# Operands of VectorE's long comparisons and products moved to PSUM, and a vector added by TensorE, in a four-layer graph network

## The chip, the cores and the metric

The kernel runs on one core of one Trainium2 chip. A core has five engines with their own instruction queues: TensorE (PE in the profile; PEld is its weight load), VectorE (DVE), ScalarE (ACT), GpSimd (POOL) and SyncE (SP). SBUF is the working memory of 128 partitions, PSUM the memory of eight banks that TensorE writes and that VectorE and ScalarE can read and write. The metric is the device time of one execution in microseconds (us); lower is better.

## The reference

Four layers of a graph network over 6250 nodes with 128 features and 100,000 edges. Edges are sorted by destination, and both ends and the relation of an edge are data of the run. Each layer takes `h = relu(layernorm(x))` and adds its result to `x`:

```python
# L0: weighted sum of the sources' rows
x = x + (1 + eps) * h + segment_sum(h[src] * edge_weight[:, None], dst)
# L1: three rounds of a gated graph convolution
h1 = relu(h @ W_node + b_node); w = (z * edge_attr).sum(1)
for i in range(3):
    agg = segment_sum(w[:, None] * (h1 @ conv[i])[src], dst)
    h1 = gru_cell(agg, h1, ...)
x = x + h1
# L2: a weight matrix per relation (16), scaled by one attention value per relation
alphas = sigmoid(relu(erps @ attn_w1 + attn_b1) @ attn_w2 + attn_b2)
vrps = zeros.at[dst].add(alphas[rels] * (h @ w_rel)[rels, src])
x = x + relu(vrps.at[dst].add((h @ update)[dst]))
# L3: mean over the edges by source (the same edges, grouped by their other end)
x = x + (h + segment_sum(h[dst], src) / max(deg, 1)) @ W.T + b
```

## The kernel before

The edges lie in 782 tiles of 128 edges (784 with padding, `ET`), the nodes in 49 blocks of 128 (`BLK`). An aggregation is a *pass*: for each tile GpSimd issues one indirect DMA that fetches the 128 source rows into one of 64 ring slots of `G` (`gather`, L709). VectorE builds a 128 x 128 selection matrix `M` from the tile's destinations (`build`, L1260 and L1262), TensorE multiplies `M` with the rows (`mm`, L813), and VectorE adds the product to the accumulator's block (`one_round`, L1282). A tile that touches two blocks takes two steps, so a pass has 832 steps in 26 rounds of 32 (`NRD`, `RD`). Every 64th tile is not gathered by GpSimd: SP fetches its 128 rows one by one (L576), so GpSimd issues 770 gathers in a pass and 780 in the last. There are six passes, one after the other: L0, three of L1 (called passes 1, 2 and 3 here), L2 and L3. Between them lie dense stages (layer norm, gates), which need the whole of a pass and give the rows that the next one gathers.

GpSimd, at every fourth tile `t`, waits until the rows of tile `t + 3 - 32` have landed (SP counts the landings, L587) and until TensorE has done step `t - 12` of the pass, which frees the ring slot (`gather_pass`). TensorE, in its queue's order, waits for SP's count, for `M` and for a free PSUM bank (banks 0 to 3).

The passes of L1 and L2 carry extra work for later layers, put between the steps by hand (`extra(r, u)`, `u` the step in its round):

- Pass 1, `place`, 98 blocks of 8 tiles, one every 8 steps. VectorE compares the chunk numbers of an iota (`srow`) with the edges' (`hs_t`) into one-hots of 128 x 392 (`one_hots`, L1429, at `u % 8 == 0`). TensorE multiplies them with a triangle to rank each edge among its like (`place`, at `u % 8 == 3`, PSUM bank 4 or 5). At `u % 8 == 6` VectorE adds the tiles' first numbers `Qb` (L1446), multiplies by the one-hots (L1448), and reduces (L1449). ScalarE's queue loads `Qb` for block `j` with one DMA that repeats a row of 392 numbers over 128 partitions (L1883), issued when VectorE has released the buffer of block `j - 2`.
- Passes 2 and 3, `places`: for every 4 tiles four comparisons of `irow`, an iota, with the numbers `hi_f` and `lo_f`, 128 x 256 each (L1457); seven times, `chunk_places` compares and multiplies in pieces of 128 x 400 (L1470, L1472).
- L2, `attention`: for 16 tiles at a time, the relations are compared with `srow[:, 0:16]` (L1602), multiplied by `alpha` (L1603) and reduced (L1604).

Of the kernel before, what the change touches and what calls it, by code (L numbers as in the profile page):

```python
# [5 lines left out]
ALU = mybir.AluOpType  # L6
# [7 lines left out]
P = 128  # L14
# [7 lines left out]
BLK = -(-N // P)  # L22
PAD_NODE = BLK * P - 1
R, B = 16, 8
# [18 lines left out]
RD = 32  # L43
NRD = S // RD
# [25 lines left out]
PB = 8  # L70
# [19 lines left out]
PASS_PLACE = PASS_L1  # L90
PASS_ORDER = {PASS_L1 + 1: (0, 4), PASS_L1 + 2: (4, NB)}
SORT_AT = 1
PLACE_AT = 1
KEY3_AT, LIST3_AT, LAST_AHEAD = 8, 14, 22
XT, XC = 3 * GN, 4
LN0, N0, G0, G1, G2, N2, N3 = range(7)
# [14 lines left out]
def gnn_kernel(nc, a, out):  # L111
# [4 lines left out]
    with ExitStack() as ctx:  # L116
        def sb(name, shape, dt=F32):
            return ctx.enter_context(nc.sbuf_tensor(name, shape, dt))
# [16 lines left out]
        ps = ctx.enter_context(nc.psum_tensor("ps", [P, 8, BANK], F32))  # L135
# [3 lines left out]
        irow = sb("irow", [P, P])  # L139
        srow = sb("srow", [P, SW])  # L140
# [175 lines left out]
        rows3 = sorting[0:T3_TB, 4 * QA * R:4 * QA * R + T3_NB * P].rearrange("p (b c) -> p b c", b=T3_NB)  # L316
        ix3_i = gate[:, 0:T3].bitcast(I32)
        adiag = sb("adiag", [R, R])
        alpha = sb("alpha", [P, R])
        note = sb("note", [P, 16])  # L320


# [13 lines left out]
        s_tr = sem("s_tr")  # L336
# [468 lines left out]
        def _(pe):  # L805
# [6 lines left out]
            def mm(dst, lhsT, rhs, start=True, stop=True):  # L812
                return nc.tensor.matmul(dst, lhsT, rhs, start=start, stop=stop, skip_group_check=True)  # L813
# [137 lines left out]
            def place(r, u):  # L951

                v = u // PB
                j = (r - PLACE_AT) * (RD // PB) + v
                if u % PB == 3 and not (isinstance(j, int) and j >= PLACES):
                    pe.wait_ge(s_oh, j + 1)
                    mm(ps[:, 4 + v % 2, 0:PB * BLK], before_b[:], oh[:, v % 2, :]).then_inc(s_rk, 1)

            def order(i, rr, u):

# [93 lines left out]
                last = mm(ps[0:R, 5, 0:D], erT[0:w, c, :], aw1[0:w, c, :], start=c == 0, stop=c == 2)  # L1054
            last.then_inc(s_tr, 1)
            unit()
            mm(ps[:, 4, 64:64 + R], ones[0:R, :], adiag[:]).then_inc(s_tr, 1)
            gather_pass(PASS_L2, 0, KEY3_AT, W1)
            staircase(2, 6, T3_TB, T3_NB, S3)
            unit()  # L1060
# [44 lines left out]
        def _(dve):  # L1105
# [160 lines left out]
            def lead_in(k, of, weight):  # L1266
                for s in range(LEAD):
                    build(k, s, s, of, weight)
# [109 lines left out]
            def lanes(t, n, m):  # L1378
                return t.rearrange("s (b c) -> s b c", c=1).broadcast_to((n, t.shape[1], m))
# [44 lines left out]

            def one_hots(j, v):
                hs = hs_t[:, bass.ds(j * PB, PB)].rearrange("p (k c) -> p k c", c=1).broadcast_to((P, PB, BLK))
                of = srow[:, 0:BLK].rearrange("p (k c) -> p k c", k=1).broadcast_to((P, PB, BLK))
                to = oh[:, v % 2, :].rearrange("p (k c) -> p k c", k=PB)
                V.tensor_tensor(to, of, hs, ALU.is_equal).then_inc(s_oh, 1)  # L1429

            def place(r, u):
                i = r - PLACE_AT
                v = u // PB
                j = i * (RD // PB) + v
                if u == 0:
                    link.turn(i, 8)
                if isinstance(j, int) and j >= PLACES:
                    return
                if u % PB == 0:
                    one_hots(j, v)  # L1440
                if u % PB == 6:
                    half = v % 2
                    at = pq[:, half, :]
                    dve.wait_ge(s_rk, j + 1)
                    dve.wait_ge(s_qld[half], 16 * (i * (RD // PB // 2) + v // 2 + 1))
                    V.tensor_tensor(at, ps[:, 4 + half, 0:PB * BLK], Qb[:, half, :], ALU.add).then_inc(s_pl, 1)  # L1446
                    dve.wait_ge(s_pl, j + 1)
                    link(V.tensor_tensor(at, at, oh[:, half, :], ALU.mult))  # L1448
                    link(V.tensor_reduce(pos_f[:], at.rearrange("p (k c) -> p k c", k=PB), AX.X, ALU.add))  # L1449
                    V.tensor_copy(pos[:, bass.ds(j * PB, PB)], pos_f[:]).then_inc(s_pos, 1)  # L1450

            def places(j, q):

                row = irow[:].rearrange("p (k c) -> p k c", k=1).broadcast_to((P, 2, P))
                for t, to, done in ((hi_f, hi_m, s_hi), (lo_f, lo_m, s_lo)):
                    for k in range(0, B4, 2):
                        ins = V.tensor_tensor(to[:, q, k:k + 2], row, lanes(t[:, bass.ds(j * B4 + k, 2)], P, P),  # L1457
                                              ALU.is_equal)
                    ins.then_inc(done, 1)
# [28 lines left out]
            for l in range(LAYERS):  # L1488
                k = PASS_L1 + l
                if k == PASS_L1 + 1:  # L1490
                    link(V.tensor_single_scalar(lo_i, pos[:], P - 1, ALU.bitwise_and))
                    V.tensor_copy(lo_f, lo_i)
                    link(V.tensor_single_scalar(pos[:], pos[:], 7, ALU.logical_shift_right))
                if k in PASS_ORDER:
                    link(V.tensor_copy(hi_f, pos[:]))
                    j = PASS_ORDER[k][0] * (TB // B4)
                lead_in(k, rel, w_l)
                if k in PASS_ORDER:
                    if j:
# [6 lines left out]
                if k == PASS_PLACE:  # L1506
                    gather_pass(k, 0, PLACE_AT, *args)
                    gather_pass(k, PLACE_AT, NRD, *args, place)
                    link.part(NRD - 1 - PLACE_AT, 8, 4)
                else:  # L1510
                    def order_and_relation(r, u, k=k):
                        order(PASS_ORDER[k][0] // 2 + r // HALF, r % HALF, u, PASS_ORDER[k][1] * (TB // B4))
                        if k == PASS_L1 + 2:
                            relation(r, u)
                            if r == FEED and u == 0:

                                link(V.tensor_copy(src_f, ix_src[:, 0:ET]))
                                link(V.scalar_tensor_tensor(ix_t, src_f, float(R), rl[:], ALU.mult, ALU.add))
                                signal(s_ix)

                    for r in range(NRD):
                        one_round(k, r, RD if r < NRD - 1 else RD - LEAD, *args, order_and_relation)
                    link.leave(1, link.k)
# [66 lines left out]
            dve.wait_ge(s_att, 2)  # L1590
            ready(V.tensor_scalar(adiag[:], ident[0:R, 0:R], alog[:, 1:2], None, ALU.mult))
            unit_done()
            link(V.tensor_copy(alpha[:], ps[:, 4, 64:64 + R]))
            link.leave(1, link.k)

            def attention(q, to):

                at = bass.ds(q * QA, QA)

                def over(t):  # L1600
                    return t.rearrange("p (s r) -> p s r", s=1).broadcast_to((P, QA, R))
                link(V.tensor_tensor(by_rel[:, to], lanes(rl[:, at], P, R), over(srow[:, 0:R]), ALU.is_equal))  # L1602
                link(V.tensor_tensor(by_rel[:, to], by_rel[:, to], over(alpha[:]), ALU.mult))  # L1603
                V.tensor_reduce(a_l[:, at], by_rel[:, to], AX.X, ALU.add).then_inc(s_aw, 1)  # L1604

            def attention_ahead(r0):
# [114 lines left out]
        def _(act):  # L1721
# [150 lines left out]
            for l in range(LAYERS):  # L1872
                ph = G0 + l
                if PASS_L1 + l == PASS_PLACE:

                    act.wait_ge(s_qrdy, 1)
                    act.dma_start(q_flat.rearrange("(b p h) -> p b h", p=TB, h=BLK), Q).then_inc(s_qst, 16)
                    act.wait_ge(s_qst, 16)
                    q_of = q_flat.rearrange("(j c) -> j c", c=PB * BLK)
                    for j in range(PLACES):  # L1880
                        if j >= 2:
                            act.wait_ge(s_pl, j - 1)
                        act.dma_start(Qb[:, j % 2, :], q_of[j:j + 1, :].broadcast_to((P, PB * BLK))) \  # L1883
                            .then_inc(s_qld[j % 2], 16)
                        if (j - 6) % 7 == 0 and 0 <= (j - 6) // 7 < NG:
                            hn_out(0, (j - 6) // 7)
                elif PASS_L1 + l == PASS_L1 + 1:
                    act.wait_ge(s_hs[1], two_stores(1, G0))
                    def every_eighth(j):
                        if j % 8 == 4 and j >= 12 and (j - 12) // 8 < NG:  # L1890
                            hn_out(1, (j - 12) // 8)

                    for v in range(*PASS_ORDER[PASS_L1 + l]):
                        order(v // 2, v % 2, every_eighth)
                elif PASS_L1 + l == PASS_L1 + 2:
                    act.wait_ge(s_hs[1], two_stores(1, G1))
                    done = []

                    def some(j):
                        n = j - PASS_ORDER[PASS_L1 + 2][0] * (TB // B4) - 12  # L1900
                        if n >= 0 and n % 8 == 0 and n // 8 < NG:
                            hn_out(2, n // 8)
                            done.append(n // 8)
                    for v in range(*PASS_ORDER[PASS_L1 + l]):
                        order(v // 2, v % 2, some)
                    for i in range(len(done), NG):
                        hn_out(2, i)
                    act.wait_ge(s_hnd, 16 * NG * LAYERS)
# [97 lines left out]
```

## Time and profile before

| | |
|---|---|
| three timed runs, us | 6528.85, 6530.85, 6519.95; median 6528.85 |
| profiled execution, first to last instruction (span) | 6527.6 us |
| GpSimd busy | 4763.4 us, 73% of the span |
| VectorE busy | 3826.2 us, 59% |
| TensorE busy | 3347.2 us, 51% |
| mean granted TensorE clock | 0.598 of full speed |

Of the profiled execution the page gives the span alone; no other time of it is listed. The busy time of an engine holds no waits, and issue of DMAs by SP and ScalarE is not counted as busy. "issue" in the chain of waits is time in which an engine waited for nothing that the profile shows.

### The profile page before, as it was taken

The page shows a single profiled execution, that of the slowest core. Times are in us where ns is not written, and L with a number is a line of the kernel's source. Part 1 is how long each engine was busy: PE and PEld are TensorE (multiplying, and loading weights), DVE is VectorE, ACT ScalarE, POOL GpSimd, SP SyncE. Part 2 cuts the span into 40 slices and gives each one's busy share as a digit, 9 for nine tenths or more (in the row PEclk, how much of TensorE's full clock was granted, in tenths as well). Part 3 has the DMA queues.
Part 4 walks back from the last instruction along what each step waited for, and adds up shares of the span by engine and source line. Part 5 has one row for each costly group of instructions (what it writes and reads, how often), then busy time and mean ns, then how long its engine had stood idle before and what let it go on. Part 6 is the DMA issues. An engine that isn't in the chain of part 4 may idle for free.

```text
span 6527.6 us, 107309 instructions
## 1 busy us (share of the span) xinstructions
PE 3347.2 (51%) x13560; PEld 2696.1 (41%) x13560; DVE 3826.2 (59%) x13371; ACT 878.1 (13%) x2206; POOL 4763.4 (73%) x5006
## 2 busy tenths in 40 slices
PE   3444445444446555555755554595454444444444
PEld 3333334333334445554454543443343333333334
DVE  6767676666666656666666664454454444444445
ACT  1000001000002111111311110143333333000000
POOL 6777776777774677777777777675777776777775
PEclk6555556555556766667767675696555555555556
DMA  5434432333332222222222222253222222222222
GB/s 141 110 107 111 111 108 78 79 78 78 81 78 76 55 57 58 57 57 58 67 57 58 57 57 59 79 222 123 54 54 53 54 54 55 54 54 55 54 55 59
DMA packets 287231, 491.20 MB, mean 75 GB/s; under 512 B 100950, under 2 KB 183899, under 8 KB 280268
## 3 DMA queue, kind: packets, MB, share of 16 engines
q0 software_dynamic: 156176, 306.05, 19.2%
q1 hardware_dynamic: 89707, 94.69, 4.4%
q10 hardware_dynamic: 40656, 83.51, 4.2%
q14 instruction: 535, 4.37, 0.2%
q8 instruction: 157, 2.57, 0.2%
HBM read 398.97 MB, written 86.91 MB: 74 GB/s over the span
## 4 chain that ended last, share of the span: by engine, by line
POOL 41%; issue 20%; DMA 13%; SPq 11%; PE 10%; DVE 3%; ACT 1%; DVEq 1%; POOLq 0%; ACTq 0%
POOL G L709 40%; DMA G<-h_rows,ix_src 10%; PE ps L813 10%; SPq L576 8%; SPq L568 3%; DMA G<-h_rows 1%; DMA G<-t_rows,pos 1%; DMA t_rows<-G 0%; DVEq L1271 0%; PE ps L875 0%; DVE HNA L1282 0%; ACT gate L1920 0%; SPq L587 0%; DVE bst L1199 0%; ACT gate L1828 0%
## 5 line engine op out<-in xcount | busy, mean ns | idle before, releaser
L709 POOL DMA_INDIRECT G<-h_rows,ix_src x3860 | 3699.8, 958 | 1284.2 <-issue 1044.2
L813 PE MATMUL ps<-G,M 128*128 x10000 | 2558.9, 421 | 3014.0 <-SPq L587 2140.6
L813 PEld LDWEIGHTS ps<-G,M 128*128 128x128 f32 x10000 | 2171.0, 310 | 3402.6 <-issue 3397.3
L1282 DVE TENSOR_TENSOR HNA<-HNA,ps 128x128 f32 (+1 forms) x3328 | 959.0, 288 | 1349.1 <-PE ps L813 1313.8
L1262 DVE TENSOR_SCALAR M<-irow,rel,w_l 128x128 f32<-128x128 f32 x3328 | 1207.9, 365 | 184.0 <-issue 177.5
L709 POOL DMA_INDIRECT G<-t_rows,pos x770 | 739.6, 961 | 260.7 <-issue 227.3
L1282 DVE TENSOR_TENSOR HTA<-HTA,ps 128x129 f32 x840 | 243.5, 290 | 518.2 <-PE ps L813 509.5
L1865 ACT ACTIVATE sorting<-sorting,pk 128x128 f32<-128x128 f32 x784 | 250.4, 390 | 1433.2 <-DVE sorting L1457 1432.4
L813 PE MATMUL ps<-sorting 128*128 128x128 f32 x1568 | 438.2, 376 | 2.0 <-issue 1.3
L1960 ACT ACTIVATE G<-G,pk 128x128 f32<-128x128 f32 x782 | 311.9, 402 | 676.6 <-DMA G<-t_rows,pos 676.1
L1282 DVE TENSOR_TENSOR X<-X,ps 128x128 f32 x832 | 239.3, 288 | 232.4 <-PE ps L813 222.5
L813 PEld LDWEIGHTS ps<-sorting 128*128 128x128 f32 x1568 | 369.6, 290 | 3.3 <-issue 3.2
L1260 DVE TENSOR_SCALAR M<-irow,rel 128x128 f32<-128x128 f32 x832 | 259.9, 317 | 49.5 <-issue 48.9
L1260 DVE TENSOR_SCALAR M<-irow,hs_t 128x128 f32<-128x128 f32 x840 | 256.7, 306 | 52.5 <-issue 51.8
L734 POOL DMA_INDIRECT by_src<-chunks,cix x224 | 226.4, 1011 | 74.1 <-issue 68.2
L813 PE MATMUL ps<-big,HTA 128*128 128x512 f32 x392 | 190.9, 618 | 10.0 <-DVE G L1561 10.0
L1852 ACT COPY HG<-ps 128x512 f32<-128x512 f32 (+1 forms) x39 | 21.5, 551 | 1047.1 <-DVE sorting L1446 883.5
L1753 ACT ACTIVATE HG<-X,nbias,rstd 128x128 f32<-128x128 f32 x74 | 30.6, 486 | 967.7 <-POOL nbias L727 967.7
L1824 ACT COPY gate<-ps 128x512 f32<-128x512 f32 (+1 forms) x26 | 14.5, 558 | 1008.4 <-PE ps L875 1008.4
L1457 DVE TENSOR_TENSOR sorting<-irow,hs_t 128x256 f32<-128x256 f32 x392 | 148.5, 420 | 0.0
L1457 DVE TENSOR_TENSOR sorting<-irow,gate 128x256 f32<-128x256 f32 x392 | 148.3, 420 | 0.2
L1561 DVE COPY G<-ps 128x512 f32<-128x512 f32 x98 | 67.8, 692 | 124.1 <-PE ps L813 95.2
(271 smaller groups left out, 2200.2 us busy)
## 6 DMA issues: line engine op xcount, KB each, us to landing
G<-h_rows SPq DMA_DIRECT2D x7680, 0.5 KB
G<-h_rows,ix_src POOLq DMA_INDIRECT x3860
t_rows<-G SPq DMA_DIRECT2D x49, 1024.0 KB, 4.1
HTA<-in_edge_attr_n ACTq DMA_DIRECT2D x50, 500.0 KB
HTA<-in_edge_attr ACTq DMA_DIRECT2D x50, 500.0 KB
G<-t_rows SPq DMA_DIRECT2D x1536, 0.5 KB
sorting<-q_flat ACTq DMA_DIRECT2D x98, 196.0 KB
G<-t_rows,pos POOLq DMA_INDIRECT x770
```

Source lines behind the costliest of these rows:

```text
L568: _, row = nc.values_load_multi_w_load_instructions(listed[32 * j:32 * j + 1, bass.ds(c * P + q * ROWS_A_QUAD, RD)], engines=[mybir.Engine ...
L576: sp.dma_start(G[e:e + 1, BY_ROW + j % 2, 0:D], table[bass.ds(row[e % RD], 1), :]) \
L709: return nc.gpsimd.indirect_dma_start(to, None, table, bass.IndirectOffsetOnAxis(ap=ix, axis=0))
L734: nc.gpsimd.indirect_dma_start(by_src, bass.IndirectOffsetOnAxis(ap=cix[:, c:c + 1], axis=0), chunks[:, v, k * CH:(k + 1) * CH], None).the ...
L813: return nc.tensor.matmul(dst, lhsT, rhs, start=start, stop=stop, skip_group_check=True)
L1260: ins = V.tensor_scalar(M[:, slot, :], irow[:], at, None, ALU.is_equal)
L1262: ins = V.tensor_scalar(M[:, slot, :], irow[:], at, weight[:, bass.ds(s, 1)], ALU.is_equal, ALU.mult)
L1282: V.tensor_tensor(to, to, ps[:, u % SLOTS, 0:n], ALU.add).then_inc(s_add, 1)
L1457: ins = V.tensor_tensor(to[:, q, k:k + 2], row, lanes(t[:, bass.ds(j * B4 + k, 2)], P, P), ALU.is_equal)
L1561: V.tensor_copy(t_buf[t % 2][:, c * BANK:(c + 1) * BANK], ps[:, 6, :]).then_inc(s_te[1], 1)
L1865: ins = A.mul(to, to, pk[:, bass.ds(j * B4 + k, 1)])
L1960: A.mul(G[:, slot, 0:D], G[:, slot, 0:D], a_l[:, bass.ds(turn * RING + u, 1)]) \
```

## The change

Constants that VectorE compared with or multiplied by from SBUF are copied to PSUM once before the pass, and the long operations read them there. In `place` the addition of `Qb` by VectorE goes: TensorE adds it with a second matrix product, of a row of ones with the one row of 392 numbers, into the same PSUM bank; the product with the one-hots then reads PSUM. `Qb` is loaded into one partition. The wait for its landing moves from VectorE to TensorE, and the signal that releases its buffer now comes with the product.

```diff
+L2_IOTA, L2_ALPHA = 448, 480
-        alpha = sb("alpha", [P, R])
@@ TensorE, place
                     pe.wait_ge(s_oh, j + 1)
-                    mm(ps[:, 4 + v % 2, 0:PB * BLK], before_b[:], oh[:, v % 2, :]).then_inc(s_rk, 1)
+                    pe.wait_ge(s_qld[v % 2], 16 * ((r - PLACE_AT) * (RD // PB // 2) + v // 2 + 1))
+                    mm(ps[:, 4 + v % 2, 0:PB * BLK], before_b[:], oh[:, v % 2, :], stop=False)
+                    mm(ps[:, 4 + v % 2, 0:PB * BLK], ones[0:1, :], Qb[0:1, v % 2, :], start=False).then_inc(s_rk, 1)
@@ TensorE, before L2's pass
-            mm(ps[:, 4, 64:64 + R], ones[0:R, :], adiag[:]).then_inc(s_tr, 1)
+            mm(ps[:, 7, L2_ALPHA:L2_ALPHA + R], ones[0:R, :], adiag[:]).then_inc(s_tr, 1)
@@ VectorE, one_hots
-                of = srow[:, 0:BLK].rearrange("p (k c) -> p k c", k=1).broadcast_to((P, PB, BLK))
+                of = ps[:, 7, 0:BLK].rearrange("p (k c) -> p k c", k=1).broadcast_to((P, PB, BLK))
@@ VectorE, place
-                    dve.wait_ge(s_qld[half], 16 * (i * (RD // PB // 2) + v // 2 + 1))
-                    V.tensor_tensor(at, ps[:, 4 + half, 0:PB * BLK], Qb[:, half, :], ALU.add).then_inc(s_pl, 1)
+                    V.tensor_tensor(at, ps[:, 4 + half, 0:PB * BLK], oh[:, half, :], ALU.mult).then_inc(s_pl, 1)
                     dve.wait_ge(s_pl, j + 1)
-                    link(V.tensor_tensor(at, at, oh[:, half, :], ALU.mult))
@@ VectorE, places
-                row = irow[:].rearrange("p (k c) -> p k c", k=1).broadcast_to((P, 2, P))
+                row = ps[:, 4, 0:P].rearrange("p (k c) -> p k c", k=1).broadcast_to((P, 2, P))
@@ VectorE, before the passes of L1
                 if k in PASS_ORDER:
+                    V.tensor_copy(ps[:, 4, 0:P], irow[:])
...
+                if k == PASS_PLACE:
+                    link(V.tensor_copy(ps[:, 7, 0:BLK], srow[:, 0:BLK]))
+                    link.leave(1, link.k)
@@ VectorE, before L2's pass, and attention
-            link(V.tensor_copy(alpha[:], ps[:, 4, 64:64 + R]))
+            link(V.tensor_copy(ps[:, 7, L2_IOTA:L2_IOTA + R], srow[:, 0:R]))
-                link(V.tensor_tensor(by_rel[:, to], lanes(rl[:, at], P, R), over(srow[:, 0:R]), ALU.is_equal))
-                link(V.tensor_tensor(by_rel[:, to], by_rel[:, to], over(alpha[:]), ALU.mult))
+                link(V.tensor_tensor(by_rel[:, to], over(ps[:, 7, L2_IOTA:L2_IOTA + R]), lanes(rl[:, at], P, R), ALU.is_equal))
+                link(V.tensor_tensor(by_rel[:, to], over(ps[:, 7, L2_ALPHA:L2_ALPHA + R]), by_rel[:, to], ALU.mult))
@@ ScalarE's queue, pass 1
-                        act.dma_start(Qb[:, j % 2, :], q_of[j:j + 1, :].broadcast_to((P, PB * BLK))) \
+                        act.dma_start(Qb[0:1, j % 2, :], q_of[j:j + 1, :]) \
                             .then_inc(s_qld[j % 2], 16)
```

The counts of the semaphore chain that `place` uses go from 8 to 4 a round with it.

## Rows read from the trace of the kernel before

**Rows 1.** The page: busy time of each engine; the chain of waits by line.
```profile
PE 3347.2 (51%) x13560; PEld 2696.1 (41%) x13560; DVE 3826.2 (59%) x13371; ACT 878.1 (13%) x2206; POOL 4763.4 (73%) x5006
...
POOL G L709 40%; DMA G<-h_rows,ix_src 10%; PE ps L813 10%; SPq L576 8%; SPq L568 3%; DMA G<-h_rows 1%; DMA G<-t_rows,pos 1%; DMA t_rows<-G 0%; DVEq L1271 0%; PE ps L875 0%; DVE HNA L1282 0%; ACT gate L1920 0%; SPq L587 0%; DVE bst L1199 0%; ACT gate L1828 0%
```

**Rows 2.** Stretches, gathers (L709) alone: from:to, us, busy us (count), clock, DMA share, GB/s.
```profile
54.00:1025.50 971.50, 735.71 (x770) 0.51 0.40 108
1074.00:2051.50 977.50, 741.83 (x770) 0.54 0.32 77
2135.00:3114.50 979.50, 743.95 (x770) 0.67 0.22 57
3195.00:4171.00 976.00, 740.58 (x770) 0.63 0.22 57
4468.00:5452.00 984.00, 746.35 (x777) 0.52 0.21 54
5506.00:6482.50 976.50, 737.73 (x780) 0.52 0.21 54
```

**Rows 3.** Line L709 in pass 1 and in L2: ns min/median/max, first and last start.
```profile
L709 POOL DMA_INDIRECT G<-h_rows,ix_src x770: 940/945/1337, 1074.8 to 2050.1; - x193
...
L709 POOL DMA_INDIRECT G<-t_rows,pos x770: 947/952/1797, 4468.4 to 5450.5; - x193
```

**Rows 4.** Instructions of the extra work by line, columns as in Rows 3, shapes last.
```profile
L1457 DVE TENSOR_TENSOR sorting<-irow,gate x392: 410/419/486, 2136.1 to 3928.1; 128x256 f32<-128x256 f32 x196
...
L1429 DVE TENSOR_TENSOR sorting<-srow,hs_t x98: 558/559/631, 1127.4 to 2035.9; 128x392 bf16<-128x392 f32 x98
...
L1446 DVE TENSOR_TENSOR sorting<-ps,sorting x98: 554/558/567, 1131.0 to 2042.0; 128x392 f32<-128x392 f32 x98
L1448 DVE TENSOR_TENSOR sorting<-sorting x98: 566/567/626, 1131.6 to 2042.6; 128x392 f32<-128x392 f32 x98
...
L1602 DVE TENSOR_TENSOR sorting<-rl,srow x49: 416/419/426, 4466.9 to 5321.3; 128x256 f32<-128x256 bf16 x49
L1603 DVE TENSOR_TENSOR sorting<-sorting,alpha x49: 424/424/452, 4467.3 to 5321.8; 128x256 f32<-128x256 f32 x49
...
L1470 DVE TENSOR_TENSOR gate<-ccol,starts x28: 567/569/572, 2269.6 to 3820.1; 128x400 f32<-128x400 f32 x28
```

**Rows 5.** Timeline, four stretches: start us, us, engine, line, what [idle before].
```profile
1149.53 0.56 DVE L1446 TENSOR_TENSOR sorting<-ps,sorting 128x392 f32<-128x392 f32 x1
1149.84 0.94 POOL L709 DMA_INDIRECT G<-h_rows,ix_src  x1 [0.30 <-PE ps L813]
...
1162.21 0.56 DVE L1429 TENSOR_TENSOR sorting<-srow,hs_t 128x392 bf16<-128x392 f32 x1
1162.33 1.27 POOL L709 DMA_INDIRECT G<-h_rows,ix_src  x1 [0.30 <-issue]
...
1166.24 0.57 DVE L1448 TENSOR_TENSOR sorting<-sorting 128x392 f32<-128x392 f32 x1
1166.40 1.21 POOL L709 DMA_INDIRECT G<-h_rows,ix_src  x1 [0.32 <-issue]
...
3918.88 0.75 DVE L1457 TENSOR_TENSOR sorting<-irow,gate 128x256 f32<-128x256 f32 x2
3919.07 1.05 POOL L709 DMA_INDIRECT G<-h_rows,ix_src  x1 [0.30 <-issue]
```

**Rows 6.** Waits in pass 1 (1074 to 2051.5): us in total, times, longest us.
```profile
PE ps L813 <- SPq L587: 403.6, 162, 6.1
...
SPq L587 <- DMA G<-h_rows,ix_src: 152.8, 178, 3.0
```

**Rows 7.** A four-byte product of 512 columns on TensorE, columns as in Rows 3.
```profile
L813 PE MATMUL ps<-big,HTA x392: 592/592/1062, 4219.0 to 4461.8; 128*128 128x512 f32 x196
```

**Rows 8.** DMA issues in pass 1: count, KB each, us from issue to landing.
```profile
q_flat<-gate ACTq DMA_DIRECT2D x1, 150.1 KB, 4.4
```

More of the change, by code:

```diff
@@ L1435, in place @@
                 if u == 0:
-                    link.turn(i, 8)
+                    link.turn(i, 4)
                 if isinstance(j, int) and j >= PLACES:
@@ L1508, in _ @@
                     gather_pass(k, PLACE_AT, NRD, *args, place)
-                    link.part(NRD - 1 - PLACE_AT, 8, 4)
+                    link.part(NRD - 1 - PLACE_AT, 4, 2)
                 else:
```

## The prediction

> **What bounds the kernel now.** I read the page first: GpSimd is the busiest engine, and its gathers at L709 are 40% of the chain of waits, TensorE's products 10% [rows 1]. Then the gathers alone, pass by pass [rows 2]: every pass takes as long as GpSimd needs for its 770 or 780 gathers. The median gather is 0.945 us [rows 3], and about 0.305 us lie between two (the bracket "[0.30 <-..." before the gathers in the timeline, whatever releaser it names [rows 5]). 770 x 1.25 is 962.5 us, and the six stretches are 971.5 to 984.0 us long. In no pass of L1 does GpSimd stop between two gathers for longer than that; in L2 it does once, to issue seven gathers of a table (777 instead of 770 in the row). So the reader is to see a metronome: what lengthens one gather lengthens the pass, and work of VectorE, TensorE or SP that does not lengthen a gather costs nothing.
>
> How much lengthens gathers is in the same rows [rows 2, 3]. Busy time less the count times the median: pass 1 741.83 - 770 x 0.945 = 14.2 us; pass 2 16.3; pass 3 12.9; L2 746.35 - 777 x 0.952 = 6.6; L3, which has no extra work on VectorE, 737.73 - 780 x 0.945 = 0.6. L0 has 8.1, and its code does not change.
>
> What does it is seen in the timeline [rows 5]. L1429 runs from 1162.21, the gather that starts at 1162.33 takes 1.27 us instead of 0.945; L1448 from 1166.24, and the gather at 1166.40 takes 1.21. In both the gather grows by the time to the end of VectorE's instruction less 0.12 to 0.15 us. L1446, as long as these [rows 4], stands in the same position before the gather at 1149.84, and that one takes 0.94. The difference is where the operands lie: L1429 and L1448 read two tensors from SBUF, L1446 reads one from PSUM. I counted over the whole trace every instruction that began 0.08 to 0.45 us before a gather and ran past its first 0.14 us: of 29 such of L1429 all 29 gathers were lengthened (0.975 us or more), of L1448 35 of 37, of L1457 118 of 122, of L1603 28 of 29, and of L1446 0 of 24.
>
> **The change part by part.** The sum is made against the profiled execution's span, 6527.6 us, 1.25 us below the median of the runs; no other time of that execution is given, so I carry the difference over.
>
> *Operands in PSUM.* Each gather longer than its pass's median by 8 ns or more I put down to the VectorE instruction that runs at its start. Pass 1: L1429 31 gathers, 6.8 us, L1448 38 gathers, 6.8 us, so 13.6 of the 14.2. Pass 2: L1457, 89 gathers, 12.6 us. Pass 3: L1457, 63 gathers, 8.5 us. L2: L1603 and L1602, 35 gathers, 3.8 us. Together 38.5 us. Not removed: `chunk_places`, in 17 gathers 4.5 us (its 56 operations, of which the row of L1470 shows half [rows 4], keep two SBUF operands), the weights of the relations (L1423, 1.0), single long operations of L2, and the builds of `M`, some 1 us in each pass. All the altered operations have after the change the operand form of L1446: first input from PSUM, second from SBUF. Bounds: 0 if the blocking comes back in the new form, 50.0 us (14.2 + 16.3 + 12.9 + 6.6) if every other cause should go as well. I take 38.5, by the nearest row, L1446, whose count was 0 of 24.
>
> The Trainium skill speaks on both sides here (SBUF — State Buffer, "Who interferes with whom"): a VectorE instruction with two SBUF inputs contends with a GpSimd instruction that reads SBUF; but the same list tells of a probe in which `tensor_tensor` did not stall a DMA that GpSimd issued, and infers that writing the descriptors needs only the port that `tensor_tensor` leaves free. By the second the sum would be 0 and the time 6528.85. The trace decides for the first: 35 of 37 gathers beside L1448 are longer.
>
> *Durations on VectorE.* An operand in PSUM changes nothing: L1446 0.558 us, L1448 0.567 [rows 4]. That the PSUM operand is one repeated along the tile (stride 0) no row shows; if it doubled the 448 operations of pass 2 (0.42 us each), VectorE would have 188 us more work in a pass of 979.5 us, where the page has it busy 59% of the span [rows 1], and GpSimd would not see it. The addition that goes (98 x 0.558 = 54.7 us) gains nothing for the same reason: GpSimd was not waiting for it.
>
> *TensorE's second product.* 98 products of 392 columns in four-byte numbers with a weight load. No row has that shape; 512 columns take 0.59 to 1.06 us [rows 7], so at most 98 x 1.06 = 104 us, beside 403.6 us in which TensorE waits for SP's count in this pass [rows 6]. Taken at 0; if that cover were gone, at most the 104 us would show.
>
> *The wait for `Qb` on TensorE.* Behind it in TensorE's queue stand the products of the pass, behind them VectorE's additions, and after 12 steps GpSimd, whose ring slots they free. The load for block j goes out when the product of block j - 2 is done, at its sixth step; TensorE needs it at the third step of block j, 13 steps later. 98 blocks from 1131.6 to 2042.6 are 9.39 us a block or 1.17 a step [rows 4], so there are 15 us. The nearest row, a DMA of 150 KB on the same queue, lands in 4.4 us [rows 8]; the new load is 1.6 KB. Cost 0; below and above: -1 us (the 98 loads of 196 KB that go had shared the DMA engines with the last gathers) to +0.
>
> *The load and its queue.* Still 98 issues on ScalarE's queue. The release now comes with the product, which stands where the addition stood, so the loads go out at the same step as before; nothing else on that queue moves.
>
> *Copies.* One of 49 columns before pass 1, one of 128 before passes 2 and 3; nearest row, by size, the additions of 128 columns, about 0.3 us. They run while the first rows are gathered; taken at 0.3 us each, 0.9 us, bounds 0 and 0.9. In L2 a copy takes the place of another.
>
> *Does anything else become late?* Without the lengthening the passes come to 963 to 970 us. SP waits 152.8 us in pass 1 for gathered rows to land [rows 6], so its queue keeps up with 14 us less. TensorE and VectorE stay below.
>
> Sum: 6527.6 - 38.5 + 0.9 = 6490.0 us of span, and 6528.85 - 37.6 = 6491 us of time.
>
> **The rivals.**
>
> 1. *Other blockers take over.* The builds of `M` (832 in a pass) and `chunk_places` still stop GpSimd at times, and gathers that are no longer stopped by the long operations meet them instead. For it: one gather of L2 took 1.797 us, 0.85 over the median [rows 3], and no attention operation is long enough for that. Against it: in L3, with only builds of `M` and additions, the excess is 0.6 us [rows 2]. If half is given back: 6528.85 - 19 = 6510 us.
> 2. *The change does not do what it says.* The second input from SBUF still takes the port when the first is a repeated PSUM operand, or the lengthening has another cause that moves along: 6529 us. The inference on the Trainium skill's page above (SBUF — State Buffer, "Who interferes with whom") would give that time too. Against it: 0 of 24 beside L1446.
> 3. *Slower: the row of `Qb` comes late.* The loop product j - 2, load, TensorE j has 15.3 us. From that point on every microsecond of landing delays each second block, 49 times in the pass. At 17.3 us: 98 us, and pass 1 would no longer be set by GpSimd, so its 13.6 us are lost too: 6528.85 - (37.6 - 13.6) + 98 = 6603 us. For it: the load reads one row into a single partition and TensorE's queue is in order. Against it: the 4.4 us row [rows 8], a margin of three.
>
> **How the numbers follow.** Forecast 0.82; rival 1 0.09; rival 2 0.05; rival 3 0.04. The range: below, 6528.85 - 50 = 6479, less a microsecond for the landing, 6478; above, rival 1's 6510 with 3 us for the spread of the runs, 6513. What lies outside is rivals 2 and 3 and a tenth of the rest. About 13 us (0.2%) can be told from no change. The forecast and rival 1 are faster by more than that, 0.91; rival 2 is the same, 0.05; rival 3 slower, 0.04.
>
> **What would show it.** In the profile after, the gathers' busy time should be near 728.5 us in pass 1, 731 to 732 in passes 2 and 3, and 742.5 in L2 (777 gathers), that of L0 and L3 as it is; the maximum of L709 in pass 1 should fall from 1.34 us to below 1.1; no gather that starts beside the altered operations may be longer than the others. TensorE's waits for the landing of `Qb` should be absent. The prediction is wrong if gathers beside PSUM-reading operations are still lengthened, or if the gaps of 0.305 us between gathers grow.

## The result, and the profile after

The changed kernel takes 6489.23 us (median of 4 runs, 6488.62 to 6490.57), the kernel before 6524.4 us in the runs beside it (4 runs, 6519.86 to 6530.85). The ratio is 0.9946 with a 95% interval of 0.9934 to 0.9958: 35.2 us less, by the interval 27 to 43. The span of the profiled execution fell from 6527.6 to 6486.8 us.

The page after: busy time of each engine, and the chain of waits by line (answering to [rows 1]).

```profile
PE 3491.4 (54%) x13756; PEld 2730.4 (42%) x13756; DVE 3764.5 (58%) x13276; ACT 878.0 (14%) x2206; POOL 4721.9 (73%) x5006
...
POOL G L709 38%; DMA G<-h_rows,ix_src 11%; PE ps L813 10%; SPq L576 9%; SPq L568 3%; DMA G<-h_rows 1%; DMA t_rows<-G 1%; DMA G<-t_rows,pos 1%; DVE HNA L1284 0%; PE ps L875 0%; DVEq L1273 0%; ACT gate L1924 0%; SPq L587 0%; DVE M L1264 0%; DVE bst L1201 0%
```

TensorE has 144 us more work, VectorE 62 us less, GpSimd, with the same 5006 instructions, 41.5 us less. The last is about what the span lost. The idle time before the gathers of nodes' rows did not change, 1284.2 us before and 1284.3 after (line and shapes, count | busy us, mean ns of one | idle us before them; the kernel before first):

```profile
L709 POOL DMA_INDIRECT G<-h_rows,ix_src x3860 | 3699.8, 958 | 1284.2 <-issue 1044.2
L709 POOL DMA_INDIRECT G<-h_rows,ix_src x3860 | 3662.6, 949 | 1284.3 <-issue 1035.2
```

Where the time was lost is in the gathers pass by pass, the columns as in [rows 2] (from:to, us, busy us and count, clock, DMA share, GB/s), each stretch again from the first gather of a pass to its last:

```profile
55.00:1025.00 970.00, 734.67 (x770) 0.52 0.39 108
1075.50:2039.00 963.50, 728.13 (x770) 0.53 0.22 58
2122.00:3088.50 966.50, 731.19 (x770) 0.68 0.22 58
3169.00:4135.50 966.50, 731.32 (x770) 0.66 0.22 58
4432.00:5412.50 980.50, 743.23 (x777) 0.51 0.21 54
5466.50:6442.00 975.50, 737.24 (x780) 0.51 0.20 54
```

Pass 1 lost 13.7 us of gathers, pass 2 12.8, pass 3 9.3, L2 3.1; L0 and L3, which were not changed, 1.0 and 0.5. The six together fell from 4446.15 to 4405.78 us, 40.4 of the 40.8 us of span. The prediction had named 728.5, 731 to 732 twice, and 742.5.

The long gathers of pass 1 are gone. Line L709 in pass 1 (ns min/median/max; before [rows 3] the maximum was 1337):

```profile
L709 POOL DMA_INDIRECT G<-h_rows,ix_src x770: 940/944/1042, 1076.2 to 2037.9; - x193
```

And positions like those in [rows 5], in the timeline after (start us, us, engine, line, what): the one-hots start 0.19 us before a gather, the comparisons 0.48 us before one and, as a second pair, 0.18 us after it began.

```profile
1171.07 0.56 DVE L1431 TENSOR_TENSOR sorting<-ps,hs_t 128x392 bf16<-128x392 f32 x1
1171.26 0.94 POOL L709 DMA_INDIRECT G<-h_rows,ix_src  x1 [0.30 <-issue]
...
2159.73 0.75 DVE L1457 TENSOR_TENSOR sorting<-ps,gate 128x256 f32<-128x256 f32 x2
2160.21 0.94 POOL L709 DMA_INDIRECT G<-h_rows,ix_src  x1 [0.30 <-issue]
2160.39 0.74 DVE L1457 TENSOR_TENSOR sorting<-ps,hs_t 128x256 f32<-128x256 f32 x2
```

Both gathers take 0.94 us. Counted as before the change (the instruction begins 0.08 to 0.45 us before a gather and runs past its first 0.14 us; a gather of 0.975 us or more is lengthened): L1431, the former L1429, 0 of 39; the product L1447 0 of 27; L1457 1 of 110; L1607, the former L1603, 0 of 26. Before, these were 29 of 29, 35 of 37, 118 of 122 and 28 of 29.

The same count in the kernel before tells two more things. VectorE's additions to the accumulator (L1282, 0.29 us) read their first input from SBUF and their second from PSUM; 233 of them stood in that position and none lengthened its gather, so it need not be the first input that lies in PSUM. The reductions of `place` (L1449) are as long as the products but have one input, in SBUF; they lengthened 0 of 21, and 0 of 33 after the change. So a long instruction that reads SBUF does no harm by that alone. Their row in the kernel before, columns as in Rows 4:

```profile
L1449 DVE TENSOR_REDUCE pos_f<-sorting x98: 560/561/564, 1132.2 to 2043.2; 128x8 f32<-128x392 f32 x98
```

The altered instructions are as long as before ([rows 4]: 0.559, 0.567, 0.419, 0.424), though the PSUM operand is repeated along the tile; columns as in Rows 4:

```profile
L1431 DVE TENSOR_TENSOR sorting<-ps,hs_t x98: 556/558/566, 1128.7 to 2023.8; 128x392 bf16<-128x392 f32 x98
...
L1447 DVE TENSOR_TENSOR sorting<-ps,sorting x98: 552/558/560, 1133.6 to 2029.8; 128x392 f32<-128x392 f32 x98
...
L1457 DVE TENSOR_TENSOR sorting<-ps,gate x392: 406/415/421, 2122.7 to 3893.4; 128x256 f32<-128x256 f32 x196
...
L1607 DVE TENSOR_TENSOR sorting<-ps,sorting x49: 423/424/426, 4431.4 to 5283.1; 128x256 f32<-128x256 f32 x49
```

TensorE's second product is dearer than was allowed for, and its cover thinner. First its row and the page's line for it (count | busy us, mean ns of one | idle before), then the waits in pass 1 (us in total, times, longest us), which answer to [rows 6]:

```profile
L813 PE MATMUL ps<-sorting,ones x196: 852/935/1017, 1129.8 to 2025.8; 1*128 1x392 f32 x196
...
L813 PE MATMUL ps<-sorting,ones 1*128 1x392 f32 x196 | 163.8, 936 | 0.0
```

```profile
PE ps L813 <- SPq L587: 219.3, 107, 5.5
...
SPq L587 <- DMA G<-h_rows,ix_src: 139.8, 189, 2.9
```

A four-byte product is two records (196 for 98 products); the page gives them 163.8 us in all, and TensorE's wait for SP's count fell from 403.6 to 219.3 us. No wait for the landing of `Qb` is among TensorE's waits, and SP still waits 140 us for gathered rows.

### The profile page after: what moved, and what is told of

Its sections match the earlier page's. It is cut to its first block, busy times and chain, and to the rows that moved or that the text cites. A ratio compares the mean times of both kernels' runs of the same rounds, so it can differ in the third digit from the quotient of the medians.

```text
span 6486.8 us, 107606 instructions
## 1 busy us (share of the span) xinstructions
PE 3491.4 (54%) x13756; PEld 2730.4 (42%) x13756; DVE 3764.5 (58%) x13276; ACT 878.0 (14%) x2206; POOL 4721.9 (73%) x5006
## 4 chain that ended last, share of the span: by engine, by line
POOL 39%; issue 20%; DMA 13%; SPq 12%; PE 10%; DVE 3%; ACT 1%; DVEq 0%; POOLq 0%; ACTq 0%
POOL G L709 38%; DMA G<-h_rows,ix_src 11%; PE ps L813 10%; SPq L576 9%; SPq L568 3%; DMA G<-h_rows 1%; DMA t_rows<-G 1%; DMA G<-t_rows,pos 1%; DVE HNA L1284 0%; PE ps L875 0%; DVEq L1273 0%; ACT gate L1924 0%; SPq L587 0%; DVE M L1264 0%; DVE bst L1201 0%
## 5 line engine op out<-in xcount | busy, mean ns | idle before, releaser
L709 POOL DMA_INDIRECT G<-h_rows,ix_src x3860 | 3662.6, 949 | 1284.3 <-issue 1035.2
L709 POOL DMA_INDIRECT G<-t_rows,pos x770 | 736.6, 957 | 260.7 <-issue 226.9
L813 PE MATMUL ps<-sorting,ones 1*128 1x392 f32 x196 | 163.8, 936 | 0.0
L1457 DVE TENSOR_TENSOR sorting<-ps,gate 128x256 f32<-128x256 f32 x392 | 146.5, 415 | 0.0
L1457 DVE TENSOR_TENSOR sorting<-ps,hs_t 128x256 f32<-128x256 f32 x392 | 145.6, 412 | 0.0
```

The lines of the kernel that those rows point to most:

```text
L709: return nc.gpsimd.indirect_dma_start(to, None, table, bass.IndirectOffsetOnAxis(ap=ix, axis=0))
```

## The experiments

The theory: a VectorE instruction with two SBUF inputs holds up a gather that starts under it, one that reads one of the two from PSUM does not, and GpSimd's gathers set the length of a pass. The rivals: the gain comes from less work and fewer bytes; VectorE's work as such delays the pass; the load of `Qb` is near to being late. Times are compared with the kernel before on the same chip.

### The edits of pass 1 alone

```diff
 (the changed kernel)
-                row = ps[:, 4, 0:P].rearrange("p (k c) -> p k c", k=1).broadcast_to((P, 2, P))
+                row = irow[:].rearrange("p (k c) -> p k c", k=1).broadcast_to((P, 2, P))
...
-                link(V.tensor_tensor(by_rel[:, to], over(ps[:, 7, L2_IOTA:L2_IOTA + R]), lanes(rl[:, at], P, R), ALU.is_equal))
+                link(V.tensor_tensor(by_rel[:, to], lanes(rl[:, at], P, R), over(srow[:, 0:R]), ALU.is_equal))
...
```

> Only the edits of pass 1 are made (one-hots and product read PSUM, TensorE adds the chunk numbers); passes 2, 3 and L2 read SBUF as before. Port theory (a VectorE instruction with two SBUF inputs holds up a gather, one with a PSUM input does not): the gathers of pass 1 are busy 728 us instead of 742, those of passes 2, 3 and L2 744, 741 and 746 as before; time 13 to 14 us under the kernel before. Rival (the gain comes from a general relief, less DMA traffic and less work on VectorE, and spreads): more than 14 us, or passes 2 and 3 change too.

6510.57 us against 6521.93, ratio 0.9983 (0.9973 to 0.9992): 11.4 us where 13 to 14 were expected; by the interval it is 5 to 18. The gathers of passes 1, 2 and 3:

```profile
1073.00:2055.00 982.00, 728.50 (x770) 0.53 0.22 60
2116.00:3116.00 1000.00, 743.94 (x770) 0.66 0.22 59
3164.00:4174.00 1010.00, 740.03 (x770) 0.65 0.22 59
```

Pass 1 is as in the changed kernel, 13.3 us under [rows 2], passes 2 and 3 as before ([rows 2]: 743.95 and 740.58). Nothing spreads.

### The comparisons of passes 2 and 3 alone

```diff
 (the kernel before)
-                row = irow[:].rearrange("p (k c) -> p k c", k=1).broadcast_to((P, 2, P))
+                row = ps[:, 4, 0:P].rearrange("p (k c) -> p k c", k=1).broadcast_to((P, 2, P))
...
                 if k in PASS_ORDER:
+                    V.tensor_copy(ps[:, 4, 0:P], irow[:])
```

> Only the comparisons of passes 2 and 3 read their iota from PSUM. No engine has less work, no byte less is moved. Port theory: gathers of pass 2 at 731 us, of pass 3 at 732 us, pass 1 at 742 as before; time 21 us under the kernel before. Rival (relief by less work and fewer bytes): no change, within 3 us.

6501.27 us against 6521.93, ratio 0.9965 (0.9951 to 0.9979): 20.7 us, 21 expected.

```profile
1073.00:2055.00 982.00, 741.81 (x770) 0.53 0.32 77
2116.00:3116.00 1000.00, 731.45 (x770) 0.70 0.22 59
3164.00:4174.00 1010.00, 731.79 (x770) 0.65 0.22 59
```

Here no engine has less work and no byte less is moved: one operand lies elsewhere, and that is worth 20.7 us. With the 11.4 of pass 1 it comes to 32.1. The intervals of these times are 6 to 9 us either way, so the 3 us of L2 rest on its gathers alone.

### TensorE's addition and the small load alone

```diff
 (the kernel before, with the second product on TensorE and Qb in one partition)
...
-                    V.tensor_tensor(at, ps[:, 4 + half, 0:PB * BLK], Qb[:, half, :], ALU.add).then_inc(s_pl, 1)
+                    V.tensor_copy(at, ps[:, 4 + half, 0:PB * BLK]).then_inc(s_pl, 1)
```

> The kernel before, with TensorE's addition and the small load of the chunk numbers alone: VectorE copies the sum from PSUM to SBUF in the place of the addition and multiplies two SBUF operands as before, and the one-hots compare two SBUF operands as before. Port theory: nothing gained, gathers of pass 1 at 741 to 743 us, time within 3 us of the kernel before. Rival (the 19 MB of loads that go, or the addition on TensorE, bring the gain of pass 1): 13 to 14 us under the kernel before.

6526.27 us against 6521.93, ratio 1.0006 (0.9997 to 1.0016): no difference that can be told from none. Pass 1:

```profile
1073.00:2055.00 982.00, 744.79 (x770) 0.52 0.22 57
```

The DMA share of pass 1 fell as in the changed kernel, from 0.32 [rows 2] to 0.22, and the gathers gained nothing: in the position counted above the one-hots lengthened 34 of 36 and the product on two SBUF operands 33 of 33. The gathers are even 3 us longer than before, where I had expected 741 to 743 us. The lengthened gathers are 67 where they were 64, so the count alone does not explain the 3 us, and no run here does.

### The addition left on VectorE

```diff
 (the changed kernel, with Qb in 128 partitions and one product on TensorE)
-                    V.tensor_tensor(at, ps[:, 4 + half, 0:PB * BLK], oh[:, half, :], ALU.mult).then_inc(s_pl, 1)
...
+                    V.tensor_tensor(ps[:, 4 + half, 0:PB * BLK], ps[:, 4 + half, 0:PB * BLK], Qb[:, half, :],
+                                    ALU.add).then_inc(s_pl, 1)
                     dve.wait_ge(s_pl, j + 1)
+                    link(V.tensor_tensor(at, ps[:, 4 + half, 0:PB * BLK], oh[:, half, :], ALU.mult))
```

> The changed kernel, but the addition stays on VectorE with the chunk numbers loaded to 128 partitions: it reads PSUM and SBUF and writes its sum back to PSUM, and the product reads that. Port theory: all of the gain is kept, gathers of pass 1 at 728 to 730 us, time 35 to 39 us under the kernel before. Rival (TensorE's addition and the smaller loads matter): pass 1 back at 742 us, time only 22 to 25 us under the kernel before.

6484.98 us against 6521.93, ratio 0.9945 (0.9928 to 0.9961): 37.0 us, all of the gain. Pass 1, with the large loads back (DMA share 0.32):

```profile
1073.00:2055.00 982.00, 728.02 (x770) 0.54 0.32 79
```

So the part of the change that TensorE does contributes nothing by itself. It is one way to have the sum in PSUM; writing it there from VectorE is another, and equal by the gathers of pass 1 (728.02 us against 728.13).

### Two more products in a block, from SBUF or from PSUM

```diff
 (the changed kernel, place on VectorE)
+                if u % PB == 2:
+                    half = v % 2
+                    V.tensor_tensor(pq[:, half, :], srow[:, 0:PB * BLK], oh[:, half, :], ALU.mult)
+                if u % PB == 4:
...
```

In the second kernel `ps[:, 7, 0:PB * BLK]` stands in the place of `srow[:, 0:PB * BLK]`.

> The changed kernel with two more products of 128 x 392 in every block of pass 1, 196 in all, at the steps between the one-hots and the product; both of their inputs lie in SBUF, their results are overwritten. Port theory: each costs GpSimd what L1429 and L1448 cost it before, 13.6 us / 196 = 0.069 us, so pass 1 rises from 728 to 741 or 742 us of gathers and the time by 13 to 14 us over the changed kernel. Rival (VectorE's work as such delays the pass): the same rise as with the same products reading PSUM.

> The same 196 products more, with the first input read from PSUM and the second from SBUF. Port theory: gathers of pass 1 stay at 728 to 729 us and the time within 3 us of the changed kernel, though VectorE has 110 us more work in the pass. Rival (VectorE's work as such): the same rise as with two SBUF inputs.

From SBUF 6503.49 us, from PSUM 6495.09, both beside 6529.73 of the kernel before: ratios 0.9961 (0.9947 to 0.9975) and 0.9948 (0.9931 to 0.9964). These times are 8.4 us apart with intervals of 9 to 11 either way, and the changed kernel was not run on this chip, so the gathers have to decide. The first kernel's pass 1:

```profile
1073.00:2055.00 982.00, 738.78 (x770) 0.53 0.21 58
```

The second's:

```profile
1073.00:2055.00 982.00, 730.93 (x770) 0.54 0.21 60
```

The second was profiled in an execution whose median gather took 0.947 us, not 0.944 (see the end), so its excess over the median is 730.93 - 770 x 0.947 = 1.7 us; the first's is 738.78 - 770 x 0.944 = 11.9, the changed kernel's 1.2. The same work therefore costs 10.7 us with two SBUF inputs and 0.5 with one in PSUM, which settles that it is not VectorE's work as such. The price was 0.055 us an instruction, not the 0.069 expected: of the first products of a block 42 lengthened a gather, of the second ones 11. In this trace of the first kernel, one such product and the gather over it:

```profile
1163.67 0.56 DVE L1445 TENSOR_TENSOR sorting<-srow,sorting 128x392 f32<-128x392 f32 x1
1163.99 1.06 POOL L709 DMA_INDIRECT G<-h_rows,ix_src  x1 [0.30 <-issue]
```

How many meet a gather depends on where in GpSimd's 1.25 us the instruction falls, so the price taken from other lines was a quarter too high here.

### A later load

```diff
 (the changed kernel, ScalarE's queue)
-                        if j >= 2:
-                            act.wait_ge(s_pl, j - 1)
+                        if j >= 1:
+                            act.wait_ge(s_pl, j)
```

> The changed kernel with the load of the chunk numbers of block j issued only when the product of block j - 1 is done, 5 steps (5.9 us) before TensorE needs them instead of 13. If a row lands in some 2 to 4 us, as I hold: TensorE does not wait longer than now by more than a microsecond here and there, pass 1 and the time stay within 2 us of the changed kernel. Rival 3 of the prediction (the load is late): every block then waits, pass 1 grows by tens of microseconds.

6497.26 us, ratio 0.9952 (0.9935 to 0.9968), within 2.2 us of the kernel with the products from PSUM run beside it, and the excess over the median (0.947) in pass 1 is 730.50 - 729.2 = 1.3 us, as in the changed kernel. TensorE's waits show no landing there either:

```profile
PE ps L813 <- SPq L587: 225.7, 114, 5.5
PE ps L813 <- DVE M L1264: 54.3, 16, 4.5
PE ps L813 <- issue: 16.8, 4, 5.3
```

With 5 steps instead of 13 the row is still there in time. Rival 3 was far off.

### More operands in PSUM

What still lengthened gathers after the change, gather by gather: in L0 5.6 us by the products of the edge weights (L1296), in passes 2 and 3 2.9 and 1.8 us by `chunk_places`, and 1.5 to 1.9 us a pass by the builds of `M`. In the first kernel ScalarE copies one operand of L0's products to PSUM and the chunk places read PSUM; in the second, run twice, the builds of passes 1 to 3 and L3 do too.

```diff
 (the changed kernel)
-                    ins = V.tensor_tensor(to, to, za[:, q, 1, d:d + EW_PIECE, :], ALU.mult)
+                    by = ps[0:EW_P, 4 + 2 * q + d // 8, d % 8 * DE:(d % 8 + EW_PIECE) * DE]
+                    ins = V.tensor_tensor(to, by.rearrange("p (c d) -> p c d", d=DE), to, ALU.mult)
...
-                link(pieces(lambda at: V.tensor_tensor(above[:, at], above[:, at], over(jump), ALU.mult)))
+                link(pieces(lambda at: V.tensor_tensor(above[:, at], jumps, above[:, at], ALU.mult)))
...
 (the second kernel: build)
-                    ins = V.tensor_scalar(M[:, slot, :], irow[:], at, weight[:, bass.ds(s, 1)],
+                    ins = V.tensor_scalar(M[:, slot, :], row, at, weight[:, bass.ds(s, 1)],
...
```

> The changed kernel with the products of L0 and the chunk places of passes 2 and 3 reading PSUM, but the builds of M left on SBUF. Port theory: 5.6 + 2.9 + 1.8 = 10 us under the changed kernel run beside it; the builds' 1.5 to 2 us a pass stay. Rival (the builds are what is left to gain and two SBUF inputs no longer matter at these counts): within 3 us of the changed kernel.

> The changed kernel with what still lengthens gathers moved as well: in L0 ScalarE copies one operand of the edge weights' products to PSUM (200 products of 125 x 256), in passes 2 and 3 the comparisons and products of the chunk places read PSUM, and in passes 1 to 3 and L3 the builds of M read their iota from PSUM. Port theory: gathers of L0 fall by 5.6 us to 729, of pass 2 by 2.9 for the chunk places, of pass 3 by 1.8, and by 1.5, 1.8, 1.9 and 1.2 for the builds in passes 1 to 3 and L3; together 16 to 17 us under the changed kernel, some 52 us under the kernel before. Builds take 0.30 to 0.35 us and none is drawn out to 0.5 any more. Rival (the builds are too short to matter and only take more time from PSUM): 8 to 11 us under the changed kernel.

> The changed kernel itself, as the measure for the two beside it on the same chip: 34 to 39 us under the kernel before. If gathers have a median of 0.947 us in this execution instead of 0.944, the span is some 14 us longer (4630 gathers) with the same excess over the median in every pass.

> The version with the builds of M reading PSUM too, again: 14 to 16 us under the changed kernel beside it, 4 to 6 us under the version without the builds.

On one chip, five rounds, the kernel before at 6520.06 us: the changed kernel 6481.94 (ratio 0.9941, 0.9927 to 0.9954), the first 6474.01 (0.9929, 0.9916 to 0.9943), the second 6469.97 (0.9925, 0.9912 to 0.9939). The medians fall by 7.9 us (10 expected) and by 4.0 more (4 to 6 expected), together 12.0 where 14 to 16 were expected. With intervals of 8 to 9 us either way the second step is plain only in the profile. On another chip the second kernel had 6481.02 beside 6529.73 (0.9926, 0.9910 to 0.9943), 48.7 us less where some 52 were expected. The first kernel's gathers in passes 1 to 3 and L3:

```profile
1070.00:2055.00 985.00, 728.55 (x770) 0.53 0.21 59
2115.00:3116.00 1001.00, 727.56 (x770) 0.68 0.21 60
3157.00:4174.00 1017.00, 729.00 (x770) 0.64 0.21 58
5446.00:6451.00 1005.00, 736.97 (x780) 0.52 0.19 54
```

The second kernel's gathers in L0, passes 1 to 3 and L3 (run beside the changed kernel):

```profile
54.00:1027.00 973.00, 730.07 (x770) 0.52 0.39 108
1070.00:2055.00 985.00, 726.62 (x770) 0.53 0.21 59
2115.00:3116.00 1001.00, 726.49 (x770) 0.70 0.21 60
3157.00:4174.00 1017.00, 727.06 (x770) 0.68 0.21 59
5446.00:6451.00 1005.00, 736.02 (x780) 0.53 0.20 55
```

770 x 0.944 is 726.9: in passes 1 to 3 less than 0.2 us is left over the median, where the first kernel had 1.7, 0.7 and 2.1. The gathers of these five stretches are 16.3 us (16 to 17 expected) below the changed kernel's 3662.6 (734.67 + 728.13 + 731.19 + 731.32 + 737.24). The builds were a blocker too, though a small one: by the count used above, those that read the iota from SBUF (L0 of this kernel) lengthened 26 of 72 gathers, those that read it from PSUM (passes 1 to 3) 0 of 381. The Trainium skill (SBUF — State Buffer, "Who interferes with whom") says that `tensor_scalar` can run in a mode that takes the ports shared with GpSimd. The trace agrees so far: with the iota in PSUM the 1.5 to 1.9 us a pass are gone. Whether it is that mode, or that the builds' numbers `rel` and `w_l` lie in SBUF beside the iota, no run separates. My expectation of the builds' length, 0.30 to 0.35 us, was wrong: the median grew by some 0.06 us from 0.341, though none is drawn out to 0.58 any more, as some were. TensorE's waits for them did not grow (206.0 us in the changed kernel, 188.2 in the second kernel on the other chip). Their line in the second kernel (count | busy us, mean ns of one | idle before them):

```profile
L1267 DVE TENSOR_SCALAR M<-ps,rel,w_l 128x128 f32<-128x128 f32 x2496 | 1010.6, 405 | 131.8 <-issue 126.1
```

## Why the prediction was right

The forecast was 6491 us, 37.6 under the median of the kernel before; measured were 6489.23, 35.2 under the median of the runs beside it. That the two times lie within 2 us is partly luck: the kernel before was 4.4 us lower in the runs beside the change than in those the forecast started from, and of the fall in gathers 3.9 us were no part of the sum (below).

- *What bounds the kernel.* Right: 40.4 of 40.8 us of span are gathers, the idle time before them is the same to 0.1 us, and no other engine's 62 us less or 144 us more shows.
- *Operands in PSUM, 38.5 us.* By the excess over the median (0.944 after, 0.952 in L2) pass 1 lost 12.9 us, pass 2 12.0, pass 3 8.5, L2 3.1, together 36.5. Pass 3 is as counted; the others are 0.6 to 0.7 below. What the prediction left out is its first rival in small: builds of `M` met some of the gathers that were free now, 1.5, 1.8 and 1.9 us after 1.1, 1.2 and 1.7. That is 1.2 us given back, where the rival had 19; the other 0.8 us of the shortfall are not accounted for.
- *The rest of the 40.4.* The median gather was 0.945 us in the profiled execution before and 0.944 after; over 3860 gathers of nodes' rows that is 3.9 us. The median fell in L0 and L3 as well, whose code did not change, and among the executions of one kernel it moves too (see the end), so I do not count it as the change's.
- *Two inputs or the port for writing.* The prediction weighed two statements of the Trainium skill's page SBUF — State Buffer ("Who interferes with whom") and held with contention for two SBUF inputs. The counts (29 of 29 to 0 of 39 at the same place, and 0.055 us for each added product from SBUF) agree. The probe in which `tensor_tensor` did not stall a DMA from GpSimd does not carry over to these gathers; whether that is because their row numbers lie in SBUF, no run shows.
- *Durations on VectorE.* Right: 0.558 us against 0.559, and the repeated operand costs nothing (0.412 and 0.415 against 0.419 in passes 2 and 3).
- *TensorE's second product.* The bound was wrong. "At most 98 x 1.06 = 104 us" took a row that counts each product twice [rows 7] as if it counted it once; the products took 163.8 us. It cost nothing to be seen: 219 us of waits for SP are left, and pass 1 is as long without it (728.02 us of gathers with the addition on VectorE).
- *The wait for `Qb`.* Right, with room: 5 steps do as well as 13.
- *TensorE's addition.* The prediction put its gain at nothing, and the two kernels that split it from the operands measured that: without the operands 1.0006, without the addition 0.9945.
- *Copies, 0.9 us.* Too small to be seen in any of the runs.

## What to carry to other kernels

Where GpSimd issues gathers back to back, look at the lengths of single gathers, not at shares of busy time: those over the median name, by the VectorE instruction that runs at their start, what holds GpSimd up. Here a constant operand copied to PSUM freed them at no price in length for two-input instructions, while taking work or bytes away from an engine that GpSimd did not wait for brought nothing. Price such a change by counting the lengthened gathers; a rate per instruction from other lines was a quarter too high.

## What was not expected of the hardware

The median gather is not the same in every execution. Of the kernels profiled here some had 0.944 us and some 0.947 with the same code; the changed kernel, profiled again, had this row for pass 1:

```profile
L709 POOL DMA_INDIRECT G<-h_rows,ix_src x770: 943/947/1042, 1078.7 to 2042.6; - x193
```

All of the distribution is moved, the minimum from 0.940 to 0.943 us. Over 4630 gathers 3 ns are 13.9 us, and that execution took 6498.28 us while the other four of the same kernel took 6480.38 to 6482.70. Its excess over its own median was 1.1 us in pass 1, where the first profile of the kernel has 1.3. The kernel with two more products from SBUF fits the other way round: its profiled execution had 0.944 us and took 6493.81 us, the other four 6501.91 to 6506.45. Why an execution has the one or the other is open, and so is whether it explains the 11 us between the runs of the kernel before; for a gain of half a per cent it means that excess over the median, pass by pass, tells more than one time.
